# A two-layer gated cross-attention and mixture-of-experts program: scatter-add in both layers, and the second layer's keys and values projected before its attention

## What is computed

```python
x = x + tanh(g_xattn[l]) * attention_l(layernorm(x), ctx, ctx)   # 16 heads of 16
x = x + tanh(g_ffn[l]) * experts_l(layernorm(x))                 # top 2 of 8
```

## Time and profile before

| What | us |
|---|---|
| Median of 3 runs (lowest to highest) | 950.31 (949.50 to 953.55) |
| The profiled execution, its own time | 947.15 |
| Its span | 945.4 |
| Constants | 0 to 4.1 |
| First attention | 4.1 to 238.5 (first row-maximum product at 28.4) |
| First route | 238.5 to 261.0 |
| First experts (23 blocks) | 261.0 to 543.5 |
| Second attention | 543.5 to 808.4 (first row-maximum product at 581.8) |
| Second route | 808.4 to 840.1 |
| Second experts (7 blocks) | 840.1 to 945.4 |

### The profile page before, as it was taken

One profiled execution on the slowest core, in us unless ns is written; L12 is line 12 of the kernel. 1 busy time (PEld: TensorE's weight loads), 2 busy tenths in 40 slices (PEclk: granted clock), 3 DMA queues, 4 the chain that ended last, 5 costly groups with the idle time before them and its releaser, 6 DMA issues. The chain is left out here.

```text
span 945.4 us, 17859 instructions
## 1 busy us (share of the span) xinstructions
PE 788.8 (83%) x7040; PEld 670.8 (71%) x7040; DVE 640.2 (68%) x1172; ACT 450.0 (48%) x648; POOL 361.9 (38%) x390
## 2 busy tenths in 40 slices
PE   5799999896359999999999837899999896329995
PEld 4666777564359999999999836666667555328995
DVE  3667777632758999999999434676677632768883
ACT  2256666542056666666665211364556552315541
POOL 8434552112153333333331088656432112331653
PEclk8979999999569999999999967797999889558998
DMA  5211111000366777667774043222211000545732
GB/s 170 65 37 39 50 49 38 24 24 23 140 203 230 245 241 249 238 235 237 240 246 160 34 135 87 59 72 56 55 47 36 24 24 13 191 155 203 222 81 34
DMA packets 49814, 111.39 MB, mean 118 GB/s; under 512 B 11970, under 2 KB 35011, under 8 KB 42051
## 3 DMA queue, kind: packets, MB, share of 16 engines
q0 software_dynamic: 13056, 65.30, 21.7%
q1 hardware_dynamic: 36674, 44.95, 15.3%
HBM read 87.08 MB, written 14.49 MB: 107 GB/s over the span
## 5 line engine op out<-in xcount | busy, mean ns | idle before, releaser
L471 DVE TENSOR_REDUCE mx_a<-ps_max_a 128x2 f32<-128x512 f32 x256 | 164.4, 684 | 65.2 <-PE ps_max_a L647 63.0
L390 ACT ACTIVATE prob_a<-ps_st_a 128x2048 f32<-128x2048 f32 x64 | 120.0, 1875 | 56.9 <-PE ps_st_a L668 56.9
L71 PE MATMUL ps_h_e<-xe_t_e,w_e 128*128 128x256 f32 x480 | 140.2, 292 | 8.2 <-DVE xe_t_e L1380 8.2
L73 PE MATMUL ps_h_e<-xe_t_e,w_e 128*128 128x256 f32 x480 | 137.3, 286 | 0.0
L72 PE MATMUL ps_h_e<-xe_t_e,w_e 128*128 128x256 f32 x480 | 137.1, 286 | 0.0
L71 PE MATMUL ps_y_e<-w_e,h_e 128*128 128x256 f32 x480 | 133.2, 277 | 0.0
L72 PE MATMUL ps_y_e<-w_e,h_e 128*128 128x256 f32 x480 | 133.0, 277 | 0.0
L73 PE MATMUL ps_y_e<-w_e,h_e 128*128 128x256 f32 x480 | 133.0, 277 | 0.0
L1310 ACT ACTIVATE hid_e<-ps_h_e,b_e 128x256 f32<-128x256 f32 x184 | 78.4, 490 | 94.4 <-PE ps_h_e L73 94.4
L864 POOL DMA_INDIRECT w_raw_w<-L_w,block_row x46 | 43.6, 947 | 164.8 <-DVE b_e L1352 81.1
L71 PEld LDWEIGHTS ps_h_e<-xe_t_e,w_e 128*128 128x128 f32 x480 | 94.8, 198 | 9.4 <-DVE xe_t_e L1380 9.4
(11 more groups left out here) (211 smaller groups left out, 1758.8 us busy)
## 6 DMA issues: line engine op xcount, KB each, us to landing
w_raw_w<-L_w SPq DMA_DIRECT2D x14, 1024.0 KB, 6.4
expert_out<-y_e SPq DMA_DIRECT2D x23, 256.0 KB, 4.7
ctx_raw_a<-ctx_t SPq DMA_DIRECT2D x16, 256.0 KB, 3.0
q_s_a<-q_c_a SPq DMA_DIRECT2D x128, 32.0 KB, 2.0
k_s_a<-k_c_a SPq DMA_DIRECT2D x128, 32.0 KB, 2.0
normalised<-xr SPq DMA_DIRECT2D x8, 256.0 KB, 2.2
normalised_weighted<-xr SPq DMA_DIRECT2D x8, 256.0 KB, 2.3
out<-x_sb SPq DMA_DIRECT2D x4, 512.0 KB, 3.0
```

The costliest lines, as they stand in the source:

```text
L71: pe.matmul(out, lhs[0], rhs[0], start=start, stop=False)
L73: return pe.matmul(out, lhs[0], rhs[1], start=False, stop=stop)
L390: act.activation(prob[n % 2][:, :, :, :], ps_st[:, :, :, :], ACT.Exp, scale=HD ** -0.5).then_inc(prob_ready, 1)
L471: dve.tensor_reduce(mx[:, q, h + 2 * j:h + 2 * j + 2], ps_max[j][:, :, :], AX.X, ALU.max).then_inc(max_done, 1)
```

## The change

**Scatter-add in both layers.** The routed weights are now computed in both routes and stored beside the normalised rows (`normalised_weighted`, 264 columns). Layer 0's attention stores x after each residual to a new DRAM tensor `x1`, layer 1's to `out` (L289, 256 KB a batch). Layer 0's experts pick the slot's weight (two small VectorE operations a block over 128x2x8 elements, for which the route builds `block_is`), ScalarE multiplies the biased output by it (`weigh`), and GpSimd adds the block's rows to `x1` by two indirect DMAs, issued two blocks later; the last two blocks' come at the end. `expert_out` with its store, the 32 gathers L258 and `combine` are gone; layer 1 loads x from `x1` instead, the first batch first. In the second route GpSimd no longer adds in SBUF: it issues four accumulating DMAs of the scaled rows to `out` (2 MB).

**Keys and values of layer 1 ahead.** They are projected with plain float32 products (4 for the keys of a batch, 4 and 2 of one row for the bias of the values) and stored to DRAM: 256 KB of keys and 512 KB of values a batch, the latter with their constant columns. Batches 0 to 4 (`KEYS_AHEAD` = 5) come in bodies 7 to 9 of the first attention, in the place of its fills; batches 5 to 7 in the first route. ScalarE evacuates them. The second attention loads compact keys, eight key slots and the values of each batch instead of projecting; its GpSimd splits no context, its VectorE evacuates no values. The first attention loads all its context and the four new operands at its start.

**Order.** The second attention has lists of its own on PE, ScalarE and VectorE. Of the memsets at the start those of `q_s`, of `mx` and a part of those of `v` are gone, in the second attention all of `v`'s.

The core of the diff, cut. Of the second attention's list on PE it shows the first half of a body, without its calls of `fill`, which stand where they stood before:

```diff
+KEYS_AHEAD = 5
...
+            def load_compact_keys(b):
+                wait(sp, k_round, 2 * (b - 1))
+                sp.dma_start(k_c[b % 2][:, :, :], next_keys[:, :, b * S:(b + 1) * S]).then_inc(kc_ld[b % 2], 16)
+
+            def load_key_slots(b):
+                wait(sp, st_ps, CH * (b - 2))
+                for g in range(HG):
+                    for u in range(OCT):
+                        sp.dma_start(k_s[b % 3][32 * g:32 * g + HD, 2 * u:2 * u + 2, :],
+                                     next_slots[g, :, u, :, b * S:(b + 1) * S]).then_inc(k_ld[b % 3], 16)
+
+            def load_values(b):
+                wait(sp, pv_ps, CH * (b - 2))
+                sp.dma_start(v[b % 3][:, :, :, :], dram["next_values"][b * P:(b + 1) * P, :].rearrange(
+                    "p (q h d) -> p q h d", q=QT, h=H)).then_inc(v_ld[b % 3], 16)
+
+            def store_ahead(j):
+                sp.wait_ge(ka_done, 2 * j + 2)
+                sp.dma_start(next_keys[:, :, j * S:(j + 1) * S], k_c[j % 2][:, :, :]).then_inc(ka_stored[j % 2], 16)
+                sp.wait_ge(va_done, j + 1)
+                sp.dma_start(dram["next_values"][j * P:(j + 1) * P, :].rearrange("p (q h d) -> p q h d", q=QT, h=H),
+                             ahead_values(j)[:, :, :, :]).then_inc(va_stored[j % 2], 16)
...
+            x_dst = dram["out" if layer else "x1"][0:N, :].rearrange("(t p) d -> p t d", p=P)
...
+                sp.wait_ge(x_done, b + 1)
+                sp.dma_start(x_dst[:, tiles, :], x[:, tiles, :]).then_inc(x_stored, 16)
...
-            def combine(b):
-                dve.wait_ge(rows_ld[b % 2], (b // 2 + 1) * (32 * QT))
-                for i in range(2):
-                    if i:
-                        dve.wait_ge(half_combined, b + 1)
-                    for q in range(QT):
-                        t = b * QT + q
-                        ins = dve.scalar_tensor_tensor(x[:, t, :], rows[b % 2][:, i, q, :], shared["weight"][i][:, t:t + 1],
-                                                       x[:, t, :], ALU.mult, ALU.add)
-                    ins.then_inc(combined if i else half_combined, 1)
...
+            def keys_ahead(j):
+                if j == 0:
+                    pe.wait_ge(next_ld, 64)
+                    pe.wait_ge(mt_ready, B)
+                wait(pe, ka_done, 2 * j)
+                ctx_j = ctx_raw[:, :, j * S:(j + 1) * S]
+                for c in range(KC):
+                    for k in range(KC):
+                        ins = pe.matmul(ps_max[0][:, c, :], wk_next[:, k, c * P:(c + 1) * P], ctx_j[:, k, :],
+                                        start=k == 0, stop=k == KC - 1)
+                ins.then_inc(ka_ps, 1)
+
+            def values_ahead(j):
+                if j == 0:
+                    pe.wait_ge(max_done, B * H)
+                wait(pe, va_done, j)
+                ctx_j = ctx_raw[:, :, j * S:(j + 1) * S]
+                for q in range(QT):
+                    for k in range(KC):
+                        pe.matmul(ps_max[1][:, q, :], ctx_j[:, k, q * P:(q + 1) * P], wv_next[:, k, :], start=k == 0, stop=False)
+                    ins = pe.matmul(ps_max[1][:, q, :], shared["one_row"][:, :], bv_next[:, :], start=False, stop=True)
+                ins.then_inc(va_ps, 1)
...
-                elif not first and b >= B - 1:
+                elif not first and b >= B - 1 and layer:
...
+            else:
+                for b in range(-3, B + 2):
+                    if is_batch(b + 1):
+                        head_scores(b + 1, 0)
+                    if is_batch(b + 2):
+                        queries(b + 2)
+                    if is_batch(b + 1):
+                        head_scores(b + 1, 1)
+                    if is_batch(b - 1):
+                        weigh_values(b - 1, 2)
+                    if is_batch(b):
+                        scores(b, 0)
+                    if is_batch(b + 1):
+                        head_scores(b + 1, 2)
+                    if is_batch(b - 1):
+                        weigh_values(b - 1, 3)
+                    if is_batch(b - 2):
+                        router_turn(b - 2)
+                    if is_batch(b + 1):
+                        head_scores(b + 1, 3)
+                    if is_batch(b):
+                        scores(b, 1)
+                    if is_batch(b - 1):
+                        turn_heads(b - 1, 1)
+                    if is_batch(b + 1):
+                        head_scores(b + 1, 4)
+                    if is_batch(b - 2):
+                        router_logits(b - 2)
+                    if is_batch(b):
+                        weigh_values(b, 0)
...
             for i in range(2):
+                if layer == 0:
+                    keys_ahead(i)
+                    values_ahead(i)
                 pe.wait_ge(tables_ready, i + 1)
                 for t in range(TT):
                     ins = pe.matmul(ps_token[:, :], is_lane[i][:, t, :], token_at[i][:, t, :], start=i == 0 and t == 0,
                                     stop=i == 1 and t == TT - 1)
             ins.then_inc(token_ps, 1)
+            if layer == 0:
+                for i in range(2, B - KEYS_AHEAD):
+                    keys_ahead(i)
+                    values_ahead(i)
...
-                    pool.tensor_tensor(x[:, tiles, :], x[:, tiles, :], xn[:, tiles, :], ALU.add).then_inc(noop_added, 1)
+                    pool.dma_start(out_dst[:, tiles, :], xn[:, tiles, :], accum_op=ALU.add).then_inc(buffers["out_added"], 16)
...
+            def weigh(b):
+                act.wait_ge(y_biased, b + 1)
+                if b >= 2:
+                    act.wait_ge(y_out[b % 2], loaded(b - 2, QT))
+                for q in range(QT):
+                    ins = act.activation(y[b % 2][:, q, :], y_raw[b % 2][:, q, :], ACT.Copy, scale=slot_weight[:, b, q:q + 1])
+                ins.then_inc(y_ready, 1)
...
+                    dve.tensor_tensor(by_expert[:, :, :], xe[b % 2][:, :, D:D + E], spread(buffers["block_is"][:, b, :], 1, QT),
+                                      ALU.mult).then_inc(picked, 1)
+                    dve.wait_ge(picked, b + 1)
+                    dve.tensor_reduce(slot_weight[:, b, :], by_expert[:, :, :], AX.X, ALU.add)
...
+                    if b >= 2:
+                        add_to_tokens(b - 2)
+                add_to_tokens(blocks - 2)
+                add_to_tokens(blocks - 1)
```

886 lines of the change are left out of this document (572 added, 314 removed).

## The result

| | us |
|---|---|
| Before, median of 20 executions (lowest to highest) | 948.73 (941.90 to 955.21) |
| Changed, median of 20 executions (lowest to highest) | 945.04 (930.34 to 947.50) |
| Ratio to before, 95% interval | 0.987 (0.984 to 0.990) |
| The profiled execution of the changed kernel, and its span | 945.49, 943.8 |

The changed kernel is faster, but by far less than the 2.7% forecast (925 for 950.31), and its executions don't agree with each other: 13 of the 20 took 944.7 to 947.5 us at a mean granted clock of 0.895 to 0.898, the other 7 took 930.3 to 941.3 at 0.905 to 0.919. The ratio in the table leaves all 13 out as disturbed; over all 20 the medians differ by 3.7 us, 0.4%. So the longer times belong to the kernel, and 0.4 to 0.6% is the fairer measure of what it gains.

The account below looks back on a forecast made before the run. TensorE was taken as the bound, its work in the second attention worth its time only if VectorE keeps up. 12 + 14 + 5.5 - 49 - 7.6 = -25.1 us on 947.15 gave 922, as a median 925; range 905 to 942.

Parts of the forecast that it names:

- The second attention, -49 forecast: Second attention: earlier start, shorter bodies and last batches, 215.5 us for 264.9.
- the clock: half of that loss stays, +2: Second attention's bodies: clock 0.93 against 1.00 in the first attention; half of that loss stays, +2 us.
- ahead work at the lower clock: Rival: products ahead in first attention's end and route run at the lower clock, all exposed; 940 us, chance 0.17.
- The first attention's end, +12 forecast: First attention's last bodies: products ahead exceed the fills, last evacuation and store awaited; +12 us, range 9 to 16.
- The price of a batch: Products ahead: 10 plain float32 products a batch at 0.42 us each, 4.2 us; bounds 2.2 and 7.6.
- The first route, +14 forecast: First route: small VectorE operations and partly exposed products ahead, 11.8 us at full clock, 20.2 at half; taken as +14.
- The first experts, +5.5 forecast: First experts: +0.5 us for the blocks and +5 for the last scatter-adds at the end.
- The end was forecast at +5: First experts' end: weighting, two scatter-adds and a landing after the last bias add; +5 us, 3 to 8.
- The blocks were forecast as fitting, +0.5: First experts' blocks: added VectorE, GpSimd and ScalarE work fits the 11.50 us period; +0.5 us, 0 to +6.
- The second route, -7.6 forecast: Second route: GpSimd's additions leave, so VectorE's slowed operation L1122 returns from 2.42 to 0.28 us; -7.6 us.
- Held VectorE: Rival, first experts: each scatter-add holds VectorE for its 1.95 us, +73 us, 998 in all; chance 0.02.
- the shorter bodies, 19.3 us: Second attention's four full bodies: 19.3 us each, between 18.5 and 19.6, so 77.2 in place of 98.6.

Follow-up runs that it names:

- the second timing: The changed kernel, unaltered, timed once more against the kernel before: 944.81 us, ratio 0.994.
- the kernel with ten transposes: Changed kernel with ten filler transposes for six between pairs of row-maximum products in body -1 of the second attention: 931.27 us, ratio 0.983 to before.
- the kernel with the route's order: On the kernel with ten transposes, first route: two sets of products ahead before the first token products, the third before the second: 937.33 us, ratio 0.990 to before.
- The run with the old lists: Changed kernel with the second attention's order lists of before, less keys and values, on PE, ScalarE and VectorE: 953.08 us, ratio 1.004 to before.

## Why the prediction was right and wrong

The direction was right. The size was not: the ratio of 0.987 gives half of the forecast gain (0.973), the 0.994 of the second timing under a quarter, and the median over all executions, 945.04, lies 3 us above the range. By its own steps:

- **The second attention, -49 forecast, -36 found.** The lengths at full clock were right in every part: start 21.3 forecast and 20.8 found; 53, 77.2 and 52 forecast and 53.4, 77.3 and 51.2 found in the kernel with ten transposes. The term that failed is "the clock: half of that loss stays, +2". Between that kernel's profile and the changed one's it measures 6.9 + 3.1 + 6.2, some 16 us in the three stretches. I had taken the clock as a share of the bodies' own fill; it is stretches of 15 to 30 us at or near the lower level, over bodies in which TensorE is busy throughout. That taking keys and values out of bodies -2 and -1 lengthened them is my reading and not shown; what brings them on stays open.
- **The rival "ahead work at the lower clock"** named the clock as the danger, in the wrong stage: the ends of the first attention ran at 0.92 and 0.95, the route at 0.75.
- **The first attention's end, +12 forecast, +16 found.** The price of a batch was low: 4.2 us forecast, and in the kernel with the route's order, with two sets back to back (TensorE, order in time)

```profile
260.76 1.97 PE L1301 MATMUL ps_k_r<-ctx_r,wk_r 128*128 128x256 f32 x8
262.57 1.03 PE L1310 MATMUL ps_v_r<-wv_r,ctx_r 128*128 128x256 f32 x4
263.53 0.69 PE L1311 MATMUL ps_v_r<-bv_r,one_row 1*128 1x256 f32 x2
264.16 1.13 PE L1310 MATMUL ps_v_r<-wv_r,ctx_r 128*128 128x256 f32 x4
265.22 0.69 PE L1311 MATMUL ps_v_r<-bv_r,one_row 1*128 1x256 f32 x2
265.84 1.99 PE L1301 MATMUL ps_k_r<-ctx_r,wk_r 128*128 128x256 f32 x8
```

  5.1 us. From start to start, the four products of the keys take 1.81 us, 0.45 each and near the forecast's 0.42; the other products of 128 rows 0.48 to 0.53; and a bias product, of one row, 0.62 to 0.63, where the forecast had 0.42. Four batches are exposed, +3.6. The keys of batch 2 ran at the lower level, 3.58 us for 1.89: +1.7, where the forecast had the clock give 1.2 back. Against that, a store of 512 KB landed in 2.6 us and not in 4.3. Batch 3 was hidden as forecast.
- **The first route, +14 forecast, +12.3 found.** The choice near the full-clock end (11.8) came out by two errors that cancel. From the first token products to the second 8.1 us pass for 4.1, +4.0 where +0.9 was forecast: the second set's keys ran at the lower level, 3.76 us for 1.97. From there to the end 9.9 us pass for 2.8, +7.2 where +9.5 was forecast, the last store landing in 2.6 us. That the sum fits is luck.
- **The first experts, +5.5 forecast, +10.1 found.** The end was forecast at +5 and came at +6.7: the last outputs wait for the block before them to land, then two issues and a landing (changed kernel, GpSimd and VectorE):

```profile
571.05 0.69 DVE L1736 TENSOR_TENSOR y_raw_e<-ps_y_e,b_e 128x512 f32<-128x512 f32 x1 [4.96 <-PE ps_y_e L74]
```

```profile
573.73 1.55 POOL L1614 DMA_INDIRECT x<-y_e,token_of  x1 [3.01 <-DMA x<-y_e,token_of]
575.59 1.55 POOL L1614 DMA_INDIRECT x<-y_e,token_of  x1 [0.30 <-issue]
```

  The blocks were forecast as fitting, +0.5, and cost +3.4: bias adds follow each other every 11.54 us where it was 11.45 (from the first to the 21st), 2 us in 23 blocks, and the first block is 1.3 later. VectorE had 1.1 us to spare a block on average, but its two small operations stand ahead of the remainder for which TensorE waits. In the kernel before it waited 0.60 us for TensorE ahead of the bias add, and now it doesn't wait there. No run tests this; it is read from the trace alone.
- **The second route, -7.6 forecast, -4.4 found.** VectorE's sum fell by 7.6 (27.48 to 19.90), and the operation of the earlier trace rows takes 0.29 there. That bears out the Trainium skill (SBUF — State Buffer, Who interferes with whom) on VectorE instructions with two SBUF inputs beside GpSimd's reads. The 3.2 that are missing are the landing of the accumulating DMAs at the block's end, which the prediction put beside the first expert block at no cost.
- **Held VectorE** did not happen: with 46 scatter-adds in that stage its blocks grew by 0.09 us, where the rival asked for 3.2. The rule of mutual blocking in the same section of the Trainium skill showed in no more than these 0.09 us.
- **Order and data flow.** The forecast took the shorter bodies, 19.3 us, from work taken out. The run with the old lists has the same work and takes 22.9, so 2.8 of 4.5 us a body come with the order (part of it as clock, 0.85 against 0.96), which the prediction named only as part of the change. That its 77.2 us for four bodies fits the kernel with ten transposes is in part luck.

## What to carry to other kernels

Removing work from a tightly tuned pipeline can lengthen or move its stretches at the lower clock; read the granted clock by windows of 10 us before and after, and compare stages at equal clock before judging an edit. When one kernel's executions spread by more than 1%, set them against their mean clock first: here one number explained nearly all of it. One edit's effect on the whole kernel can then have either sign (the route's order: 6 us lost beside one kernel, 14 won beside another), so look at its own stage as well. An asynchronous transfer is only hidden up to the next barrier, so ask of every DMA what the end of its block waits for, and what else is on the DMA engines by then.
